# A fused Mamba and mixture-of-experts kernel: the order of the work between the last scan and the first expert tile

## The chip, the cores and the metric

The kernel runs on 1 core of one Trainium2 chip. The metric is the device time of one execution in microseconds (us). The five engines are TensorE (PE), VectorE (DVE), ScalarE (ACT), GpSimd (POOL) and SyncE (SP), which issues most of the DMAs. Each works through its own queue of instructions in program order, and they are tied together by semaphores.

## The reference

The input x is 2 x 2048 x 128 in fp32. Cut to what matters:

```python
# layer 1: Mamba block, with residual, then LayerNorm
h  = layernorm(x) * gamma + beta
u, z = split(h @ in_proj.T)                       # 256 channels each
uc = silu(causal_conv4(u) + conv_b)
dt, Bm, Cm = split(uc @ x_proj.T)
delta = softplus(dt @ dt_proj.T + dt_proj_b)
state = exp(delta * A) * state + delta * Bm * uc   # scan over 2048 steps, 256 x 16 states
y  = (state * Cm).sum(-1) + uc * D
x1 = layernorm(x + (y * silu(z)) @ out_proj.T + x)
# layer 2: mixture of experts, top 2 of 8, with residual, then LayerNorm
p  = softmax(x1 @ Wg + bg);  p_k, idx_k = top_k(p, 2)
eo = gelu(x1 @ W1[e] + b1[e]) @ W2[e] + b2[e]
out = layernorm(x1 + sum_k p_k * eo[idx_k])
```

## The kernel before, in words

The 4096 tokens are cut into 8 units of 512 (4 groups of 128 rows). The Mamba part runs as 8 "hosts", one for each unit: function `host(j)` exists once for each engine, and each engine's copy is its own instruction order written out by hand. In host j the scan of unit j is the backbone, 32 steps of 128 x 512, four to a quad; hung between its steps are the projections of later units and the back part of earlier ones.

**The scan's own loop.** SP spreads `du` into `flow` (L371); PE spreads delta into four banks (L805); ACT turns them into decays (L1136); DVE multiplies the inflow (L1378) and scans (L1395, 128 x 512 a step); POOL multiplies two finished steps with C in one instruction, `times_c` (L554, `hc`), so that a host has 16 such "slots" on POOL; PE adds the states up (`add_states`, L814). The last state of a unit feeds `post` on DVE (L1403), `out_proj` on PE (L828), `residual` and `back_stats` on DVE (L1409, L1304, L1308), `back_rstd` on POOL (L518 to L523), `xns` on ACT (L1146), `xn_T` on PE (L837), `xnT_evac` on ACT (L1152) and `logits` on PE (L844).

**Routing.** `best_two` (L1421 to L1431) and `one_hots` (L1437, L1443) on DVE find the two experts of each row; `shift_ex` (L571, POOL) and `gate_exp` (L1156, ACT) prepare the gate's softmax; `ranks` on PE (L858, L860) and on DVE (L1450, L1453) counts the rows ahead of each one; `mask_ranks` (L577, POOL), `place` (L1457 to L1463, DVE) and `places` (L582, POOL) make each row's place in an expert's list. `tag_rows` (L584 to L594, POOL) writes four numbers behind each row: its index (L589), its first expert (L590), its first probability (L591) and the difference of the two (L592, L594). Of these only the last three instructions need the exponentials' sum, `erec`. `list_rows` (L596 to L603, POOL) then scatters 128 rows into the lists `xs` in DRAM with one indirect DMA (L601); a unit needs eight. The one before it, `carrier` (L600), is there for its waits.

In host j the lists of unit j-2 are written after slots 11, 12, 13 and 14, two at each, and `back_rstd(j-1)` stands behind slot 8. After the last host come, on POOL, the routing and lists of unit 6 (with `back_rstd(7)` between the fourth and the fifth list), then those of unit 7. On DVE the order after the last scan is `ranks(6)`, `place(6)`, `post(7, 1)`, `residual(7)`, and so on to `place(7)`, and behind it 14 small `plan` instructions (L1526 to L1541) that turn the counts into a table of 71 tiles. On PE it is `add_states`, `ranks(6)`, `out_proj(7)`, `xn_T(7)`, `logits(7)`, `ranks(7)`.

**Experts.** 71 tiles of 128 rows follow. SP loads the weights W1 of three tiles ahead (L460), then waits for all lists to be in DRAM and loads the rows (L466): six tiles of rows are issued before the W1 of the fourth. For each tile PE transposes it (L988), multiplies by W1 (`hidden`, L995), ACT takes Gelu (L1279), PE multiplies by W2 (`output`, L1003), DVE scales, POOL scatters the result (L680). PE runs `x_T(n)`, `hidden(n-1)`, `output(n-2)` in turn. The first Gelu carries an ACT_TABLE_LOAD, since exponentials used another table before. A final part of 8 units adds the two halves and normalizes.

**Filling matmuls.** `idle` (L698) and `keep_busy` (L850) are matmuls on constants (128 x 512 bf16) whose result nobody reads; there are 36 and 130 of them, all before the last host.

Of the kernel before, what the change touches and what calls it, by code (L numbers as in the profile page):

```python
# [6 lines left out]
ACT = mybir.ActivationFunctionType  # L7
# [65 lines left out]
def mamba_moe(nc, consts, bcsel, du_d, xs, results, x, ln_gamma, ln_beta, in_proj_w, conv_w, conv_b, x_proj_w,  # L73
              dt_proj_w, dt_proj_b, A_log, Dskip, out_proj_w, Wg, bg, W1, b1, W2, b2, out):
    with ExitStack() as ctx:
# [34 lines left out]
        ones = sb("ones", [P, P], BF16)  # L110
# [19 lines left out]
        scrap = sb("scrap", [P, TT])  # L130
# [373 lines left out]
        def _(pool):  # L504
# [64 lines left out]
            def shift_ex(u):  # L569
                pool.wait_ge(s_top, u + 1)  # L570
                nc.gpsimd.tensor_tensor(ex[:], top[:], top[:, :, 0:1].broadcast_to([P, TT, E]), ALU.subtract)\  # L571
                    .then_inc(s_exs, 1)

            def mask_ranks(u):
                pool.wait_ge(s_rk, u + 1)
                for k in range(2):
                    ins = nc.gpsimd.tensor_tensor(masked[:, k], oh[:, k], rank[:], ALU.mult)  # L577
                ins.then_inc(s_ma, 1)
# [2 lines left out]
                pool.wait_ge(s_pf, u + 1)  # L581
                nc.gpsimd.tensor_copy(pos[u % 2][:], posf[:]).then_inc(s_po, 1)  # L582

            def tag_rows(u):  # L584
                pool.wait_ge(s_xn, u + 1)
                pool.wait_ge(s_er, u + 1)
                pool.wait_ge(s_ti, u + 1)
                row = xn[u % 2]
                nc.gpsimd.tensor_scalar(row[:, :, D], idc, float(T * u), None, ALU.add).then_inc(s_row, 1)  # L589
                nc.gpsimd.tensor_copy(row[:, :, D + 1], topi[:, :, 0]).then_inc(s_row, 1)  # L590
                nc.gpsimd.tensor_tensor(row[:, :, D + 2], ex[:, :, 0], erec[:], ALU.mult).then_inc(s_row, 1)  # L591
                nc.gpsimd.tensor_tensor(second[:], ex[:, :, 1], erec[:], ALU.mult).then_inc(s_row, 1)  # L592
                pool.wait_ge(s_row, 5 * u + 4)
                nc.gpsimd.tensor_tensor(row[:, :, D + 3], second[:], row[:, :, D + 2], ALU.subtract).then_inc(s_row, 1)  # L594
# [10 lines left out]
            def host(j):  # L605
                late = j + 1 < UNITS
                for slot in range(2 * QUADS):
                    times_c(QUADS * j + slot // 2, slot % 2)
                    if slot == 12 and j + 3 < UNITS:
                        front_rstd(j + 3)  # L610
                    if j == 0 and slot == 1:
                        front_rstd(2)
                    if slot == 7 and late and j >= 1:
                        add_log(j + 1)
                    if slot == 9 and late:
                        less_negative(j + 1)
                    if slot == 10 and late:
                        delta_u(j + 1)
                    if slot == (5 if j else 7) and late:
                        relu_plus_exp(j + 1)  # L620
                    if j >= 2:
                        if slot == 1:
                            shift_ex(j - 2)
                        if slot == 3:
                            mask_ranks(j - 2)
                        if slot == 6:
                            places(j - 2)
                            tag_rows(j - 2)
                        if slot in (11, 12, 13, 14):
                            first_row = 2 * (11, 12, 13, 14).index(slot)  # L630
                            list_rows(j - 2, first_row)
                            list_rows(j - 2, first_row + 1)
                    if slot == 8 and j >= 1:
                        back_rstd(j - 1)
# [23 lines left out]
                host(j)  # L658
            last = UNITS - 1
            shift_ex(last - 1)  # L660
            mask_ranks(last - 1)
            places(last - 1)
            tag_rows(last - 1)
            for n in range(TT):
                list_rows(last - 1, n)
            back_rstd(last)
            for n in range(TT, 2 * TT):
                list_rows(last - 1, n)
            shift_ex(last)
            mask_ranks(last)  # L670
            places(last)
            tag_rows(last)
            for n in range(2 * TT):
                list_rows(last, n)

# [19 lines left out]
        def _(pe):  # L695
# [125 lines left out]
            def out_proj(u, ts):  # L821
                mbank = fbank[fill_of(u, "out") % 2]
                if 0 in ts:
                    front_bank(u, "out")
                    pe.wait_ge(s_yd, 2 * u + 2)
                for t in ts:
                    for h in range(HALVES):
                        ins = nc.tensor.matmul(mbank[:, P * t:P * t + P], yg[:, h, P * t:P * t + P], woutT[:, h, :],  # L828
                                               start=(h == 0), stop=(h == 1))
                if TT - 1 in ts:  # L830
                    ins.then_inc(s_ff, 1)
# [20 lines left out]
            def ranks(u):  # L852
                o = front_bank(u, "ranks")
                pe.wait_ge(s_tk, u + 1)
                for t in range(TT + 1):
                    oo = o[:, E * t:E * t + E]
                    for s in range(t):
                        ins = nc.tensor.matmul(oo, ones[:], taken[:, s, :], start=(s == 0), stop=(t == TT and s == TT - 1))  # L858
                    if t < TT:
                        nc.tensor.matmul(oo, below[:], taken[:, t, :], start=(t == 0), stop=True)  # L860
                ins.then_inc(s_ff, 1)

            def host(j):
                late, early = j + 1 < UNITS, j + 2 < UNITS
                for g in range(STEPS):
                    if g % 2 == 0:
                        spread_pair((STEPS * j + g) // 2)
                    if g >= 11 and g % 4 == 3:
                        add_states(QUADS * j + (g - 11) // 4)
                    if g in (3, 7) and j >= 1:  # L870
                        add_states(QUADS * j + (g - 11) // 4)
                    if g == 28:
                        add_skip(j, 1)
                    if j == 0:
                        first_host(g)
                        if g == 31:
                            spread_b(1)
                        continue
                    if late:
                        if g == 1:  # L880
                            proj_dt(j + 1, 0)
                        if g == 2:
                            proj_dt(j + 1, 1)
                        if g == 4:
                            spread_c(j + 1)
                    if g == 5 and j >= 2:
                        ranks(j - 2)
                    if early:
                        if g == 6:
                            xhat_T(j + 2)  # L890
                        if g in (8, 9, 10, 12):
                            conv_u(j + 2, 0, ((8, 9, 10, 12).index(g),))
                    if g == 13:
                        add_skip(j, 0)
                    if g == 14:
                        out_proj(j - 1, (0, 1))
                    if g == 16:
                        out_proj(j - 1, (2, 3))
                    if early:
                        if g in (17, 18, 20, 21):  # L900
                            conv_u(j + 2, 1, ((17, 18, 20, 21).index(g),))
                        if g == 22:
                            proj_z(j + 2, 0)
                        if g == 24:
                            proj_z(j + 2, 1)
                    if g == 25:
                        xn_T(j - 1)
                    if g == 28:
                        logits(j - 1)
                    if early:  # L910
                        if g == 29:
                            proj_x(j + 2, (0,))
                        if g == 30:
                            proj_x(j + 2, (1,))
                    if late and g == 31:
                        spread_b(j + 1)
                    if early and g in KEPT_BUSY:
                        times, what, ahead = KEPT_BUSY[g]
                        keep_busy(fill_of(j + ahead, what), times)
# [57 lines left out]
            add_states(QUADS * UNITS - 2)  # L977
            add_states(QUADS * UNITS - 1)
            ranks(last - 1)
            out_proj(last, (0, 1, 2, 3))  # L980
            xn_T(last)
            logits(last)
            ranks(last)

            def x_T(n):
                pe.wait_ge(e_g[n % 8], 16 * (n // 8 + 1))
# [34 lines left out]
        def _(act):  # L1021
# [249 lines left out]
            xns(last)  # L1271
            xnT_evac(last)
            gate_exp(last)

            def gelu(n, e):
                act.wait_ge(e_h, n + 1)
# [18 lines left out]
        def _(dve):  # L1295
# [209 lines left out]
            for j in range(UNITS):  # L1505
                host(j)
            last = UNITS - 1
            ranks(last - 1)
            place(last - 1)
            post(last, 1)  # L1510
            residual(last)
            back_stats(last)
            best_two(last)
# [137 lines left out]
```

## Time and profile before

| | us |
|---|---|
| three executions | 778.39, 779.25, 782.07; median 779.25 |
| the profiled execution | 782.08, its span 780.3 |
| DVE, PE, POOL busy | 662.5, 602.2, 577.6 |
| last scan ends | 559.88 |
| first transpose of an expert tile | 601.66 |
| first result tile added at the end (L1590) | 754.38 |

The profiled execution is 1.8 us longer than its span, which is what lies outside the first and the last instruction. Times of the trace count from the span's start. In the timeline, a line stands for instructions of one kind that follow each other: start, duration of the whole group, engine, source line, operation, output and inputs with their sizes, how many, and in brackets how long the engine was idle before it and what ended that.
### The profile page before, as it was taken

What the parts mean: (1) busy time and instruction counts of PE and PEld (TensorE: products, weight loads), DVE (VectorE), ACT (ScalarE), POOL (GpSimd) and SP (SyncE); (2) the same over time, 40 slices, a digit from 0 to 9 for tenths busy, and PEclk for the clock granted to TensorE, in tenths of its full rate; (3) what the DMA queues carried; (4) which work ended last, traced back from release to release, by engine and by line L of the source; (5) the groups of instructions that cost most, each with busy time, mean ns of one, the idle gap of its engine ahead of it and who ended that gap; (6) DMA issues with size and microseconds to landing.
All of it is one profiled execution on the core that took longest, in us unless ns stands there. A gap on an engine that the chain in (4) does not pass through costs nothing. (4 is left out here: it accounts for less than half of the span.)

```text
span 780.3 us, 11886 instructions
## 1 busy us (share of the span) xinstructions
PE 602.2 (77%) x3071; PEld 293.7 (38%) x3071; DVE 662.5 (85%) x1343; ACT 434.3 (56%) x892; POOL 577.6 (74%) x544
## 2 busy tenths in 40 slices
PE   9768888987987888898798676685431999999920
PEld 4322222322322322232232122121131999998920
DVE  4288999999999999999998999999633788886855
ACT  3758587578467576657746644334110656554625
POOL 4345787976999899899899989968765456664644
PEclk9889999999999999999999987767755999999975
DMA  3095386577669668657656764954003677776754
GB/s 94 17 226 136 81 188 162 122 164 160 142 158 256 138 150 202 144 122 180 145 135 140 164 155 103 209 127 104 25 29 114 183 204 203 216 209 171 197 166 175
DMA packets 51169, 117.34 MB, mean 150 GB/s; under 512 B 8816, under 2 KB 25008, under 8 KB 43040
## 3 DMA queue, kind: packets, MB, share of 16 engines
q1 hardware_dynamic: 45344, 107.20, 56.4%
q0 software_dynamic: 4320, 8.99, 3.6%
q8 instruction: 26, 0.43, 0.3%
q10 hardware_dynamic: 1440, 0.40, 0.2%
q14 instruction: 39, 0.32, 0.2%
HBM read 100.21 MB, written 16.35 MB: 149 GB/s over the span
## 5 line engine op out<-in xcount | busy, mean ns | idle before, releaser
L554 POOL TENSOR_TENSOR hc<-hs,Crep 128x1024 f32<-128x1024 f32 x128 | 301.1, 2359 | 72.3 <-DVE hs L1395 51.3
L1395 DVE TENSOR_TENSOR_SCAN hs<-bank,state,flow 128x512 f32<-128x512 f32 x256 | 312.8, 1267 | 15.7 <-ACT bank L1136 7.5
L1136 ACT ACTIVATE bank<-bank,negA 128x512 f32<-128x512 f32 x256 | 164.6, 660 | 168.2 <-PE bank L805 158.8
L805 PE MATMUL bank<-delta,sel 64*128 64x512 f32 x512 | 157.5, 694 | 85.5 <-DVE hs L1395 83.6
L1378 DVE TENSOR_TENSOR flow<-flow,bank 128x2048 f32<-128x2048 f32 x63 | 142.8, 2266 | 0.0
L1279 ACT ACTIVATE flow<-bank,b1T 128x128 f32<-128x128 f32 x284 | 81.2, 369 | 58.0 <-issue 31.1
L805 PEld LDWEIGHTS bank<-delta,sel 64*128 64x128 f32 x512 | 42.3, 201 | 179.0 <-DVE hs L1395 149.3
L680 POOL DMA_INDIRECT results<-flow,idn x71 | 70.0, 985 | 33.1 <-issue 31.3
L814 PE MATMUL bank<-hc,kc 128*32 128x512 f32 x512 | 73.2, 646 | 10.8 <-POOL hc L554 10.8
L995 PE MATMUL bank<-flow 128*128 128x128 f32 x568 | 78.6, 283 | 1.9 <-DVE flow L1546 1.6
L1003 PE MATMUL bank<-w_sb,flow 128*128 x568 | 76.0, 277 | 1.6 <-ACT flow L1279 1.3
L601 POOL DMA_INDIRECT xs<-xn,pos x64 | 64.0, 1001 | 16.0 <-issue 15.9
L995 PEld LDWEIGHTS bank<-flow 128*128 128x128 f32 x568 | 71.4, 197 | 3.4 <-DVE flow L1546 2.0
L742 PE MATMUL bank<-hT,wtapT 128*128 128x512 f32 x128 | 69.1, 657 | 2.8 <-ACT hT L1040 1.5
L1003 PEld LDWEIGHTS bank<-w_sb,flow 128*128 128x128 f32 x568 | 69.9, 194 | 2.2 <-issue 2.2
L679 POOL TENSOR_TENSOR carrier<-kc 128x1 f32<-128x1 f32 x71 | 13.2, 186 | 35.3 <-DVE flow L1573 22.5
L742 PEld LDWEIGHTS bank<-hT,wtapT 128*128 128x128 f32 x128 | 22.2, 197 | 41.5 <-issue 33.9
L1546 DVE COPY flow<-bank 128x128 f32<-128x128 f32 x71 | 20.7, 292 | 19.0 <-PE bank L988 13.0
L850 PE MATMUL bank<-idle_rhs,ones 128*128 128x512 bf16 x130 | 33.3, 382 | 2.8 <-ACT pre L1050 1.2
L988 PE MATMUL bank<-ident,xg 128*128 128x128 f32 x71 | 19.9, 280 | 18.1 <-DMA xg<-xs 18.1
L1566 DVE TENSOR_TENSOR flow<-bank,b_rep 128x128 f32<-128x128 f32 x71 | 20.6, 291 | 13.8 <-PE bank L1003 9.1
L814 PEld LDWEIGHTS bank<-hc,kc 128*32 128x32 f32 x512 | 10.4, 111 | 56.8 <-issue 38.9
(198 smaller groups left out, 806.3 us busy)
## 6 DMA issues: line engine op xcount, KB each, us to landing
flow<-du_d SPq DMA_DIRECT2D x63, 1024.0 KB
flow<-L_ffn_W SPq DMA_DIRECT2D x71, 256.0 KB
xg<-xs SPq DMA_DIRECT2D x71, 66.0 KB
du_d<-du SPq DMA_DIRECT2D x28, 128.0 KB
xin<-L_attn_x SPq DMA_DIRECT2D x8, 256.0 KB, 3.3
hs<-results SPq DMA_DIRECT2D x8, 256.0 KB, 4.4
out<-hc SPq DMA_DIRECT2D x8, 256.0 KB, 2.0
results<-flow,idn POOLq DMA_INDIRECT x71
```

What stands on the lines that cost most here:

```text
L554: nc.gpsimd.tensor_tensor(hc[:, Q % 2, two, :], hs[:, Q % 2, two, :], Crep[u % 3][:].unsqueeze(1).broadcast_to([P, 2, T]), ALU.mult).then_ ...
L601: nc.gpsimd.indirect_dma_start(out=xs, out_offset=bass.IndirectOffsetOnAxis(ap=pos[u % 2][:, n:n + 1], axis=0), in_=xn[u % 2][:, n % TT, : ...
L680: nc.gpsimd.indirect_dma_start(out=results, out_offset=bass.IndirectOffsetOnAxis(ap=idn[:, n % 8:n % 8 + 1], axis=0), in_=ybuf[:, n % 8, : ...
L742: ins = nc.tensor.matmul(o[:], wtapT[:, h, k, :], hT[u % 2][:, k:k + T], start=(k == 0), stop=(k == TAPS - 1))
L805: ins = nc.tensor.matmul(dbank[2 * odd + i][:], sel[rows, odd, q % 4, :], delta[u % 2][rows, q // 4, :])
L814: ins = nc.tensor.matmul(ybank[32 * j:32 * j + 32, :], fold[:, q % 4, :], hc[:, Q % 2, j, :], start=(q % 4 == 0), stop=(q % 4 == 3))
L995: ins = nc.tensor.matmul(h_bank[n % 2][:, P * k:P * k + P], w1r[n % 4][:, P * k:P * k + P], xTs[:, n % 2, :])
L1003: ins = nc.tensor.matmul(o_bank[n % 2][:, 0:D], hTs[:, n % 2, k, :], w2_sb[:].rearrange("p e k d -> p (e k d)")[:, bass.ds(e * (HK * D) + ...
L1136: nc.scalar.activation(dbank[G % 4][:], dbank[G % 4][:], ACT.Exp, scale=negA[:, ch:ch + 1]).then_inc(s_ex, 1)
L1279: ins = nc.scalar.activation(hTs[:, n % 2, k, :], h_bank[n % 2][:, P * k:P * k + P], ACT.Gelu, bias=b1T[:, bass.ds(e * HK + k, 1)])
L1378: nc.vector.tensor_tensor(flow[Q % 3][:], flow[Q % 3][:], Brep[:].unsqueeze(1).broadcast_to([P, 4, T]), ALU.mult).then_inc(s_bu, 1)
L1395: nc.vector.tensor_tensor_scan(hs[:, Q % 2, j, :], dbank[G % 4][:], flow[Q % 3][:, j, :], state[:, Q // QUADS % 2, Q % QUADS, j:j + 1], AL ...
```

## The change

Six edits, each in the hand-written order of one engine:

- POOL: `tag_rows` is cut in two. `name_rows` (index and first expert) waits for `s_xn` and `s_ti`; `weigh_rows` (probabilities) waits for `s_er`. In the hosts they stand one behind the other as before; after the last host `name_rows` moves ahead of `mask_ranks`.
- POOL: in the last host alone (`late` is false) the lists stand behind slots 8 to 11, not 11 to 14. The two lists of slot 8 come ahead of `back_rstd`.
- DVE: after the last scan `post(last, 1)` stands ahead of `ranks(last - 1)` and `place(last - 1)`.
- PE: `idle_tail` issues 5 filling matmuls ahead of the last `out_proj`, 30 ahead of `xn_T(last)`, and 64 behind `ranks(last)`, ahead of the first tile. They wait for nothing and write a bank that nobody reads then.
- ACT: behind the last `gate_exp` a Gelu of four numbers a partition, which nobody reads.

```diff
-            def tag_rows(u):
+            def name_rows(u):
                 pool.wait_ge(s_xn, u + 1)
-                pool.wait_ge(s_er, u + 1)
                 pool.wait_ge(s_ti, u + 1)
                 row = xn[u % 2]
                 nc.gpsimd.tensor_scalar(row[:, :, D], idc, float(T * u), None, ALU.add).then_inc(s_row, 1)
                 nc.gpsimd.tensor_copy(row[:, :, D + 1], topi[:, :, 0]).then_inc(s_row, 1)
+
+            def weigh_rows(u):
+                pool.wait_ge(s_er, u + 1)
+                row = xn[u % 2]
                 nc.gpsimd.tensor_tensor(row[:, :, D + 2], ex[:, :, 0], erec[:], ALU.mult).then_inc(s_row, 1)
...
-                            tag_rows(j - 2)
-                        if slot in (11, 12, 13, 14):
-                            first_row = 2 * (11, 12, 13, 14).index(slot)
+                            name_rows(j - 2)
+                            weigh_rows(j - 2)
+                        listing = (11, 12, 13, 14) if late else (8, 9, 10, 11)
+                        if slot in listing:
+                            first_row = 2 * listing.index(slot)
...
             shift_ex(last - 1)
+            name_rows(last - 1)
             mask_ranks(last - 1)
             places(last - 1)
-            tag_rows(last - 1)
+            weigh_rows(last - 1)
...
             shift_ex(last)
+            name_rows(last)
             mask_ranks(last)
             places(last)
-            tag_rows(last)
+            weigh_rows(last)
...
+            def idle_tail(times):
+                for _ in range(times):
+                    nc.tensor.matmul(dbank[3][:], ones[:], idle_rhs[:])
...
             ranks(last - 1)
+            idle_tail(5)
             out_proj(last, (0, 1, 2, 3))
+            idle_tail(30)
             xn_T(last)
             logits(last)
             ranks(last)
+            idle_tail(64)
...
             gate_exp(last)
+            act.wait_ge(s_scrap, 2)
+            nc.scalar.activation(scrap[:], minus_half[:], ACT.Gelu).then_inc(s_scrap, 1)
...
             last = UNITS - 1
+            post(last, 1)
             ranks(last - 1)
             place(last - 1)
-            post(last, 1)
```

## Rows read from the trace of the kernel before

**Rows 1.** The page, the span in 40 slices of 19.5 us: the granted clock.

```profile
PEclk9889999999999999999999987767755999999975
```

**Rows 2.** Timeline of the last host, 530 to 563 us: POOL, and DVE's one-hots and last scan.

```profile
530.40 2.34 POOL L554 TENSOR_TENSOR hc<-hs,Crep 128x1024 f32<-128x1024 f32 x1 [0.67 <-DVE hs L1395]
...
534.71 2.36 POOL L554 TENSOR_TENSOR hc<-hs,Crep 128x1024 f32<-128x1024 f32 x1
...
546.33 2.34 POOL L554 TENSOR_TENSOR hc<-hs,Crep 128x1024 f32<-128x1024 f32 x1 [0.27 <-DVE hs L1395]
...
551.12 2.36 POOL L554 TENSOR_TENSOR hc<-hs,Crep 128x1024 f32<-128x1024 f32 x1
...
555.62 2.77 DVE L1437 TENSOR_TENSOR oh<-kc,topi 128x64 f32<-128x64 f32 x1
555.94 2.36 POOL L554 TENSOR_TENSOR hc<-hs,Crep 128x1024 f32<-128x1024 f32 x1
...
558.61 1.27 DVE L1395 TENSOR_TENSOR_SCAN hs<-bank,state,flow 128x512 f32<-128x512 f32 x1
```

**Rows 3.** Timeline, the one-hots of an earlier host, beside no multiplication on POOL.

```profile
435.37 0.20 DVE L1437 TENSOR_TENSOR oh<-kc,topi 128x64 f32<-128x64 f32 x1
```

**Rows 4.** Timeline behind the last scan, 563 to 570 us.

```profile
563.17 1.94 PE L814 MATMUL bank<-hc,kc 128*32 128x512 f32 x8 [8.56 <-POOL hc L554]
...
565.88 0.46 POOL L577 TENSOR_TENSOR masked<-oh,rank 128x32 f32<-128x32 f32 x2 [2.57 <-DVE rank L1450]
...
566.51 0.68 DVE L1403 TENSOR_TENSOR yg<-bank,gated 128x512 f32<-128x512 f32 x1
566.66 0.19 POOL L582 CAST pos<-posf 128x8 uint32<-128x8 f32 x1 [0.32 <-DVE posf L1463]
...
567.34 3.75 PE L828 MATMUL bank<-woutT,yg 128*128 128x128 f32 x16 [1.77 <-DVE yg L1403]
567.40 0.20 POOL L591 TENSOR_TENSOR xn<-ex,erec 128x4 f32<-128x4 f32 x1
...
568.86 1.08 POOL L601 DMA_INDIRECT xs<-xn,pos  x1 [0.48 <-issue]
```

**Rows 5.** The chain that ended last, 577 to 603 us: start, duration, what.

```profile
577.57 1.10 PE bank L837 x4
...
581.31 0.20 DVE lg L1421
...
583.77 0.20 DVE rank L1450
...
584.85 0.17 POOL pos L582
...
587.96 1.08 POOL xs L601
...
600.56 1.69 DMA xg<-xs
```

**Rows 6.** Timeline of the last unit's logits and of the first expert tiles.

```profile
579.42 1.85 PE L844 MATMUL bank<-wg_sb,xnT 128*128 128x8 f32 x8 [0.77 <-ACT xnT L1152]
...
602.57 2.03 PE L995 MATMUL bank<-flow 128*128 128x128 f32 x8
...
604.64 0.33 SPq L460 DMA_DIRECT2D flow<-L_ffn_W  x1
604.71 1.28 ACT L1279 ACT_TABLE_LOAD   x1 [22.22 <-PE bank L995]
...
607.29 1.15 PE L1003 MATMUL bank<-w_sb,flow 128*128 x8 [0.78 <-ACT flow L1279]
```

**Rows 7.** Timeline, four transposes, six filling matmuls and eight logits elsewhere, at clock 1.00.

```profile
9.85 0.66 PE L717 MATMUL bank<-ident,xhat 128*128 128x128 f32 x4
10.35 1.46 PE L698 MATMUL bank<-idle_rhs,ones 128*128 128x512 bf16 x6
...
548.31 0.95 PE L844 MATMUL bank<-wg_sb,xnT 128*128 128x8 f32 x8
```

## The prediction

> **What bounds the kernel now.** I read the slices first: the granted clock is high through most of the program, sags from 0.8 to 0.5 towards the end of the Mamba part, and is back at 0.9 for the experts [rows 1]. Then the chain that ended last: between the last scan and the first expert tile it is one thread through PE, DVE, POOL and ACT, then eight lists on POOL, the landing and the first row load [rows 5]. Nothing overlaps there that matters, so what leaves this thread leaves the time. Then the timeline, in three parts: the last host, where POOL's multiplications stand in line with its lists [rows 2]; the stretch from the last added states to the lists of unit 6, where POOL and PE run side by side [rows 4]; and the first tiles, where PE works at 1.2 GHz and waits for a table load [rows 6]. Behind them PE paces 71 tiles and none of the edits touches it. So only the stretch 530 to 608 us is costed.
>
> **1. Lists three slots sooner.** Prices: a multiplication 2.36; two lists 551.12 - (546.33 + 2.34) = 2.45 [rows 2]; the first pair with its carrier I take as 0.3 more; `back_rstd` 534.71 - 532.74 = 1.97 [rows 2]. From slot 8 at 530.40 I add: slot 8 to 532.8, its lists to 535.5, `back_rstd` to 537.4, slot 9 to 539.8, lists to 542.2, slot 10 to 544.6, lists to 547.0, slot 11 to 549.4, lists to 551.9, then slots 12, 13, 14 back to back to 554.2, 556.6 and 558.9. If nothing else held slot 15 it would end at 561.3 where it now ends at 563.1, when PE can add the last states [rows 4], a gain of 1.8. But slot 15 needs the last scan, and before the last scan DVE has the one-hots. They cost 0.20 on their own [rows 3], and 2.77 here: recorded from 555.62, they end at 558.39, just behind the multiplication that POOL began at 555.94, 0.3 us after them [rows 2]. POOL kept a DVE instruction with two SBUF inputs out although DVE was first on record. In the new order slots 13 and 14 run back to back over exactly this moment. If POOL keeps DVE out until it has to stop, the one-hots end at 559.1, the one-hots' sum takes 0.2, the last scan (1.27 [rows 2]) ends at 560.6, and slot 15 at 563.0: gain 0.1. Bounds: 0 and 1.8. I take 0.1, because the row shows POOL winning against an earlier DVE instruction, and put 1.8 with the rivals.
>
> The Trainium skill (SBUF — State Buffer, section "SBUF: two separate sides") states that the shared port pair is an exclusive lock and that whichever of the two starts first gets it for its whole instruction. The blocking agrees with the trace (2.77 against 0.20); "first" does not by the recorded starts. By the page the waiting one-hots would go in when slot 13 ends, and the sum would be 1.7 better; that is the first rival.
>
> The two lists and their DMAs also pass `back_rstd(6)`: it ends at 537.4, 2.7 later than 534.7, and ACT's `xns(6)` (at 536.69 before) follows 0.7 later, with one decay behind it. The scan that needs this decay started 0.8 after it; I cost this at 0, and at 0.7 if that cover is gone.
>
> **2. `post` first, `name_rows` first (unit 6).** POOL sits idle for 2.57 before the masks [rows 4], so the two `name_rows` instructions cost nothing there. From `pos` to the third tag instruction it is 567.40 - 566.66 = 0.74 now, and 0.28 without the two: 0.46 off. `post` (0.68) goes ahead of the ranks on DVE; it can start when the states are added at 563.17 + 1.94 = 565.1, while the masks were released by a rank that ended 565.8, so the rank is now written at 566.1 and POOL's path starts 0.3 later. Net for the lists of unit 6: -0.15. On the other side `yg` is ready at 565.9, but PE now has 5 fillers first, 2.1 us at 1.2 GHz (0.43 each, twice the 0.216 of 2.4 GHz: six take 1.46 [rows 7], one alone 0.38, so five steps 1.08). `out_proj` starts at 567.7, 0.35 late; if the clock rises half way through it ends near 570.4, 0.7 early; without a rise 0.35 late. That hardly matters: `back_rstd` stands behind four lists on POOL, whose end moves only by 0.15, and moves with it. Term: -0.15, bounds 0 and -0.3.
>
> **3. Fillers before `xn_T`.** It starts at 577.57 [rows 5]. 30 x 0.216 = 6.5 from 570.4 ends at 576.9, before 577.4 when the rows are there; if the clock rises only at 572 they end at 578.2. Cost 0, bound +0.8. What they give: four transposes 0.66 instead of 1.10, -0.43; eight logits 0.95 instead of 1.85, -0.90 [rows 5, 6, 7]. Ranks perhaps 0.1. Term: -1.4, bounds +0.8 and -1.5.
>
> **4. `name_rows` ahead for unit 7.** From `pos` (584.85) to the first list (587.96) it is 3.1 [rows 5]. Unhindered, without the two, it would be 0.28 + (568.86 - 567.40) = 1.74 [rows 4]. DVE's plan instructions run beside it from here on, and one with two SBUF inputs can hold POOL as POOL held the one-hots: I take 2.1. Term -1.0, bounds -0.8 and -1.4. The first two tags now sit beside the ranks, where POOL waits.
>
> To the first tile: 0.1 + 0.15 + 1.4 + 1.0 = 2.6 sooner. The lists themselves (1.27 apart, eight) and the DMAs stay. SP's own work, the eight tails and W1, moves with the plan, 2 us sooner too, and is off the thread.
>
> **5. The table and the clock at the first tile.** The table load of 1.28 [rows 6] moves into ACT's idle 22.22. At 1.2 GHz PE is busy with `hidden(1)` until 606.5 and idle only 0.78 before `output(0)` [rows 6], so the table alone gives 0.8. With the clock high as well: eight products take 0.9 (1.15 recorded at the high clock, with its fixed part, against 2.03 for `hidden(0)` [rows 6]), so `hidden(0)` ends at 603.4, Gelu (1.3, from the table load's end at 605.99 to 607.29) at 604.7, `hidden(1)` at 604.4, and `output(0)` runs 604.7 to 605.6. Now it runs 607.29 to 608.2 [rows 6]. Term -2.55. It needs the clock high at the tile. The 64 fillers are 13.8 us at 2.4 GHz; the ranks end 583.7 [rows 5] - 1.5 = 582.2, so they end at 596.0, and the tile comes at 599.1: 3 us of idle PE, less if part of them ran at 1.2 GHz. I take the full term, bound -0.8. Next in line is SP: the W1 of tile 3 is issued behind six row loads, at 604.64 [rows 6], and is needed now at about 607.6 (two tiles of 1.9 behind 605.6, less the first product) and not 610.2; enough for one transfer that took 1.69 for a quarter of the bytes [rows 5], with little to spare.
>
> **Sum.** -2.6 - 2.5 = -5.1. Against the profiled execution's own 782.08 that is 777.0. That run lies 2.8 above the median of 779.25, and nothing in this stretch explains it, so I take the sum off the median: 774.1.
>
> **The rivals.**
> - **The one-hots slip in between slots 13 and 14.** For it: two engines ask for a port and one has waited a microsecond. Against: [rows 2]. A further -1.7: 772.4. Chance 0.27.
> - **The clock falls again before the first tile.** For it: in the profile before it fell while PE waited for POOL at the end of the last host, 8.56 idle [rows 4], and it stays at 0.5 in the slices of the lists [rows 1]; 3 us of idle stand between the fillers and the tile. Only the table's 0.8 is left of 2.55: 775.9. Chance 0.25.
> - **Slower: the fillers run at 1.2 GHz throughout.** Then 30 take 12.9 from 571.5 and hold `xn_T` to 584.3, 6.8 late; the 64 take 27.4 and end near 618, 16 after the first tile could start: 779.25 + 16 - 0.8 = 794.5. It turns to a loss from the point where the 64 last longer than the roughly 17 us between ranks and tile. Against: the same matmuls ran at 0.216 at the start. A milder form, one late rise at each place, costs about 2 and lands at 776.5. Chances 0.04 and 0.09.
>
> The Trainium skill (TensorE: Matmul & The Clock Gate, "Wait — 56ns, not 53.3ns?") gives 426.7 ns cold and 215.7 ns warm between such matmuls; the second agrees with the 0.216 of [rows 7].
>
> **How the numbers follow.** The forecast itself has 0.35. A measurement of this kernel can tell about 0.5%, 3.9 us, so faster means under 775.4. Of the forecast 0.85 is under it, of the first rival nearly all, of the second two fifths, of the mild late rise a quarter: 0.30 + 0.26 + 0.10 + 0.02 = 0.68. Slower than 783.1 is the full filler case and a little: 0.05. The rest, 0.27, is the same. The range goes from the first rival with the tags at their best, 770.9, to the second with `xn_T` held up and no rise in the logits, 777.5.
>
> **What would show it.** Right: the last `hc` ends within 0.2 of 563.1 and the one-hots last over 3 us; `xn_T` starts near 577.4 with logits at 0.95; from `pos` to the first list 2.1; the first tile near 599; its `hidden` at clock 1.00 and no table load behind it. Wrong: fillers that end after the rows are there, at either place; an idle PE behind the third tile waiting for W1; slots 12 to 15 that end at 561.3; a `hidden` of 2 us again.

## The result, and the profile after

The changed kernel takes 775.96 us (median of 13 runs, 774.21 to 779.22); the kernel before takes 782.07 (median of all its 13 runs). The two medians lie 6.1 us apart. One of the executions of the kernel before, at 803.29, was a slow one; the ratio, 0.9932 with a 95% interval of 0.9916 to 0.9949, leaves it out, and that is 5.3 us less. A second series of the same kernel gave 0.9942 (0.9925 to 0.9959), 4.5 us less. The forecast was 5.1 us less, and 774.1 with a range of 770.9 to 777.5.

The page of the changed kernel, the slices that answer to [rows 1]:

```profile
PEclk9889999999999999999999986857878999999975
```

The two slices of 0.5 that covered the way to the first expert tile are gone; what remains low lies inside the last hosts and in one stretch between the fillers.

The timeline of its last host, which answers to [rows 2]:

```profile
529.73 2.34 POOL L554 TENSOR_TENSOR hc<-hs,Crep 128x1024 f32<-128x1024 f32 x1 [0.76 <-DVE hs L1411]
...
551.24 6.94 POOL L554 TENSOR_TENSOR hc<-hs,Crep 128x1024 f32<-128x1024 f32 x3
...
554.97 3.31 DVE L1453 TENSOR_TENSOR oh<-kc,topi 128x64 f32<-128x64 f32 x1
...
558.41 1.28 DVE L1411 TENSOR_TENSOR_SCAN hs<-bank,state,flow 128x512 f32<-128x512 f32 x1
...
559.77 2.34 POOL L554 TENSOR_TENSOR hc<-hs,Crep 128x1024 f32<-128x1024 f32 x1 [1.59 <-DVE hs L1411]
```

Slots 12, 13 and 14 run without a gap, 6.94 for three. The one-hots of DVE, issued at 554.97, end at 558.28, which is 0.1 behind the end of the third of them. The end of slot 13, at 555.8, fell into their wait and did not let them in. Then comes the last scan, and POOL waits 1.59 for it.

The timeline behind the last scan, which answers to [rows 4]:

```profile
562.39 0.24 POOL L588 TENSOR_SCALAR xn<-kc 128x4 f32<-128x4 f32 x1
...
564.17 0.69 DVE L1419 TENSOR_TENSOR yg<-bank,gated 128x512 f32<-128x512 f32 x1 [4.48 <-PE bank L821]
...
565.83 0.19 POOL L582 CAST pos<-posf 128x8 uint32<-128x8 f32 x1 [0.32 <-DVE posf L1479]
...
566.51 2.94 PE L835 MATMUL bank<-woutT,yg 128*128 128x128 f32 x16
...
567.43 1.08 POOL L604 DMA_INDIRECT xs<-xn,pos  x1 [0.48 <-issue]
...
569.29 6.42 PE L872 MATMUL bank<-idle_rhs,ones 128*128 128x512 bf16 x29
...
572.38 0.23 POOL L518 TENSOR_SCALAR cveps<-cmv 128x4 f32<-128x4 f32 x1
...
576.15 0.63 PE L844 MATMUL bank<-ident,xn 128*128 128x128 f32 x4 [0.43 <-ACT xn L1160]
```

The first `name_rows` instruction sits in POOL's idle time at 562.39. From `pos` to the first list it is 1.60 (2.20 before [rows 4]). `out_proj` takes 2.94 for 3.75, since the clock rises inside it. The 30 fillers (one is missing from this trace, as from the 64 below) end at 575.7, 0.43 ahead of the transposes, so they hold nothing up, and the four transposes take 0.63 at the high clock.

The chain that ended last, which answers to [rows 5]:

```profile
578.61 0.20 DVE lg L1437
...
581.07 0.20 DVE rank L1466
...
582.13 0.19 POOL pos L582
...
582.48 0.39 POOL second L595
...
583.98 1.23 POOL xs L604
...
593.10 2.93 DMA xs<-xn,pos
...
597.38 1.84 DMA xg<-xs
```

From `pos` to the first list it is 1.85 for 3.1, and POOL was held up once on the way (`second` 0.39). The last scatter's landing takes 2.93, which nobody had forecast; in the chain of the kernel before the same piece took 2.28.

The timeline of the fillers and the first tiles, which answers to [rows 6]:

```profile
579.93 1.28 ACT L1289 ACT_TABLE_LOAD   x1
...
580.89 16.31 PE L872 MATMUL bank<-idle_rhs,ones 128*128 128x512 bf16 x63
...
598.32 0.33 PE L1002 MATMUL bank<-ident,xg 128*128 128x128 f32 x1 [1.12 <-DMA xg<-xs]
...
599.44 1.06 PE L1009 MATMUL bank<-flow 128*128 128x128 f32 x8
...
600.65 2.18 ACT L1295 ACTIVATE flow<-bank,b1T 128x128 f32<-128x128 f32 x8 [19.22 <-PE bank L1009]
...
601.93 1.15 PE L1017 MATMUL bank<-w_sb,flow 128*128 x8 [0.43 <-ACT flow L1295]
```

The table load stands at 579.93 under idle time. The fillers take 16.31 and not the 13.8 of the high clock. The stretches of the changed kernel show why (the clock is the third number from the right):

```profile
572.00:578.00 6.00, 4.80 (x27) 2.47 (x25) 0.00 (x0) 2.23 (x5) 4.92 (x8) 1.00 0.10 34
...
580.00:585.00 5.00, 4.48 (x24) 1.87 (x25) 3.92 (x14) 1.42 (x2) 3.09 (x10) 0.50 0.08 23
...
587.00:598.00 11.00, 10.15 (x47) 4.41 (x45) 0.86 (x4) 0.00 (x0) 5.54 (x6) 1.00 0.50 147
```

The clock fell behind the logits, during TensorE's wait for the routing (the last product ends at 578.57, and the granted clock is 0.50 from 579.0), and rose again under the fillers (1.00 from 585.75). They ended about 1.1 ahead of the first transpose, and `hidden(0)` ran at 1.06.

**One ruler for all kernels.** What lies behind the first output product differs between executions of one and the same kernel: 173.0 and 170.1 us in two profiles of the kernel before, 173.3 and 168.4 in two of the changed one. So the edits are read from the stretch between the start of slot 8 in the last host and the first output product, which repeats within 0.1. Its parts, from the starts in the timelines: A slot 8 to the end of slot 15; B from there to `xn_T(7)`; C to `lg`; D to the first list of unit 7; E first to last list; F to the first tile's transpose; G to the first output product.

| kernel | A | B | C | D | E | F | G | sum |
|---|---|---|---|---|---|---|---|---|
| before | 32.72 | 14.45 | 3.74 | 6.65 | 8.98 | 4.72 | 5.63 | 76.89 |
| before, again | 32.74 | 14.46 | 3.74 | 6.65 | 8.98 | 4.71 | 5.68 | 76.96 |
| changed | 32.38 | 14.04 | 2.46 | 5.37 | 9.12 | 5.22 | 3.61 | 72.20 |
| changed, again | 32.34 | 14.01 | 2.46 | 5.37 | 9.12 | 5.26 | 3.58 | 72.14 |

The change gives 4.7 us here: 0.34 in A, 0.41 in B, 1.28 in C, 1.28 in D and 2.02 in G, less 0.14 in E and 0.50 in F.

### The profile page after: what moved, and what is told of

Same layout as the page of the kernel before. It is cut to its first block and busy times, and to the rows that moved or that the text cites. A ratio compares the mean times of both kernels' runs of the same rounds, so it can differ in the third digit from the quotient of the medians.

```text
span 775.2 us, 12066 instructions
## 1 busy us (share of the span) xinstructions
PE 620.2 (80%) x3151; PEld 298.5 (39%) x3170; DVE 662.5 (85%) x1343; ACT 434.5 (56%) x893; POOL 576.5 (74%) x544
## 5 line engine op out<-in xcount | busy, mean ns | idle before, releaser
L821 PE MATMUL bank<-hc,kc 128*32 128x512 f32 x512 | 74.8, 659 | 9.6 <-POOL hc L554 9.6
L1009 PE MATMUL bank<-flow 128*128 128x128 f32 x568 | 75.6, 276 | 2.3 <-issue 2.1
L1009 PEld LDWEIGHTS bank<-flow 128*128 128x128 f32 x568 | 69.0, 192 | 3.4 <-issue 2.8
L857 PE MATMUL bank<-idle_rhs,ones 128*128 128x512 bf16 x115 | 29.9, 380 | 5.5 <-ACT relu L1102 1.7
L1589 DVE SCALAR_TENSOR_TENSOR flow<-xg,is_first,flow 128x128 f32<-128x128 f32 x71 | 24.9, 351 | 2.7 <-DVE flow L1586 0.2
```

Of the source, the lines that this page charges most:

```text
L821: ins = nc.tensor.matmul(ybank[32 * j:32 * j + 32, :], fold[:, q % 4, :], hc[:, Q % 2, j, :], start=(q % 4 == 0), stop=(q % 4 == 3))
L1009: ins = nc.tensor.matmul(h_bank[n % 2][:, P * k:P * k + P], w1r[n % 4][:, P * k:P * k + P], xTs[:, n % 2, :])
```

## The experiments

Ratios are to the kernel before, in interleaved runs, each series on one chip. Sums and parts are those of the ruler; the changed kernel has 72.20 and 72.14.

**The kernel before, once more** (no edit).

> The kernel before, once more, as a profile taken beside the next three. Both theories: from the end of slot 15 to the first output product 44.2 us, as in the first profile of it (607.29 - 563.12), the clock at 0.50 there; only the part behind the first tiles may differ, if that is what makes the totals of the two chips differ by 5 us.

Measured: 44.22 from slot 15 to the first output product (607.84 - 563.62), and all seven parts within 0.05. Behind it, 170.1 for 173.0. The ruler holds for the stretch that the edits touch; the totals differ elsewhere.

**The changed kernel, once more** (no edit).

> The changed kernel once more, beside the next three. Both theories: ratio to the kernel before 0.993, slot 8 to slot 15's end 32.4 us, from there to the first output product 39.8.

Measured: ratio 0.9942 (0.9925 to 0.9959), parts within 0.04 of the first profile.

### Who holds the last scan

**The one-hots behind the last scan.**

```diff
-                    if g == 30 and j == UNITS - 1:
+                    if g == 31 and j == UNITS - 1:
                         one_hots(j - 1)
```

> The changed kernel with the one-hots of unit 6 behind the last scan on DVE, not ahead of it. Theory (POOL's back-to-back multiplications keep DVE's one-hots out, and so hold the last scan and slot 15): the last scan ends some 3 us sooner, slot 15 follows slot 14 without a gap, so the 1.59 us in which POOL waited go: 1.6 us faster than the changed kernel, ratio to the kernel before 0.991. The one-hots are then held until slot 15 ends, 2 to 5 us long, and cost nothing, because TensorE needs them only behind the last added states. Rival (the last scan is late for another reason, the decay or a buffer): slot 15 ends where it did, 12.4 us behind the start of slot 12's neighbour as in the changed kernel, gain under 0.3 us.

Measured: ratio 0.9916 (0.9896 to 0.9936); A 30.71 for 32.34 to 32.38; sum 70.48. Its timeline:

```profile
552.44 9.23 POOL L554 TENSOR_TENSOR hc<-hs,Crep 128x1024 f32<-128x1024 f32 x4
...
557.36 4.40 DVE L1453 TENSOR_TENSOR oh<-kc,topi 128x64 f32<-128x64 f32 x1
...
561.73 1.94 PE L821 MATMUL bank<-hc,kc 128*32 128x512 f32 x8 [2.66 <-POOL hc L554]
```

Four slots now follow each other in 9.23, and the one-hots are held for 4.40, over the end of slot 14 (559.4) and until slot 15 ends (561.68). This hurts nobody. The theory's 1.6 is there (1.65), the rival is out.

**POOL waits for the one-hots.**

```diff
+                    if slot == 14 and not late:
+                        pool.wait_ge(s_oh, UNITS - 1)
                     times_c(QUADS * j + slot // 2, slot % 2)
```

> The changed kernel, but POOL waits for the one-hots ahead of slot 14 of the last host. If a waiting GpSimd lets the port go, the one-hots enter as slot 13 ends and take about 0.2 us beyond it; the last scan then ends 2 us sooner and slot 15 starts directly behind slot 14: POOL loses 0.3 us at the wait and wins 1.6, so 1.3 us faster than the changed kernel. Rival (the one-hots are slow by themselves in this place, not held by POOL's stream): they still last 3 us or more, slot 14 starts 1.6 us late, and slot 15 ends no sooner, or 1 us later.

Measured: ratio 0.9915 (0.9896 to 0.9933); A 30.94, 1.42 less than the changed kernel. Its timeline:

```profile
550.98 4.64 POOL L554 TENSOR_TENSOR hc<-hs,Crep 128x1024 f32<-128x1024 f32 x2
...
554.73 0.98 DVE L1455 TENSOR_TENSOR oh<-kc,topi 128x64 f32<-128x64 f32 x1
...
555.79 4.66 POOL L554 TENSOR_TENSOR hc<-hs,Crep 128x1024 f32<-128x1024 f32 x2 [0.17 <-DVE oh L1455]
```

The same one-hots in the same place, issued at the same point of POOL's stream, last 0.98 and end 0.1 behind slot 13, because POOL stops there. So an added wait takes 1.4 us out of A. It was POOL's unbroken stream that kept the port, and not the one-hots' own length. The sum is 71.36, only 0.8 under the changed kernel, since F is 5.70 and G 3.77. In G something of the prediction's second rival shows: the fillers ended 2.52 ahead of the tile, the granted clock was 1.00 until 599, 0.57 from 599 to 600 and 0.50 behind it, and the first output product took 1.86 for 1.15.

**The lists behind slots 11 to 14 again.**

```diff
-                        listing = (11, 12, 13, 14) if late else (8, 9, 10, 11)
+                        listing = (11, 12, 13, 14)
```

> The changed kernel with the last host's lists behind slots 11 to 14 again. Theory (the one-hots' wait for the port swallows what the earlier lists gain): slot 15 ends no more than 0.4 us later than in the changed kernel, measured from the start of slot 8, and the total is 0 to 0.4 us longer. Rival (the earlier lists work as meant): 1.6 us or more longer.

Measured: ratio 0.9947 (0.9930 to 0.9963); A 32.73, 0.37 longer than the changed kernel. The theory's bound of 0.4 holds. The sum is 72.73; beside A, F is 0.3 longer (5.57, see below) and G 0.1 shorter.

**Lists late and one-hots behind.** Both edits above.

> The last host's lists behind slots 11 to 14 and the one-hots behind the last scan. Theory (two limits, each hiding the other: with late lists slot 15 waits for POOL's lists, with early lists for the last scan): the last scan ends 2.8 us sooner but slot 15 still stands behind two lists, so it ends where it did in the kernel with late lists, within 0.3 us, and the 1.3 to 1.6 us that the same move gave with early lists are absent. Rival (moving the one-hots is worth something by itself): 1 us or more faster than with late lists alone.

Measured: ratio 0.9924 (0.9907 to 0.9942); A 32.70, as with late lists alone. Its timeline:

```profile
557.33 2.44 DVE L1411 TENSOR_TENSOR_SCAN hs<-bank,state,flow 128x512 f32<-128x512 f32 x2
...
562.65 0.96 POOL L604 DMA_INDIRECT xs<-xn,pos  x1 [0.31 <-issue]
563.64 2.35 POOL L554 TENSOR_TENSOR hc<-hs,Crep 128x1024 f32<-128x1024 f32 x1
```

The last scan is done at 559.77 and slot 15 begins at 563.64, directly behind a list. The move that gives 1.65 with early lists gives 0.03 with late ones; early lists give 0.37 with the one-hots in the old place and 1.99 (32.70 - 30.71) with them behind. The sum, 71.84, is 0.9 under that of late lists, all of it in F (4.74 for 5.57), which is not what was moved.

### What the fillers and the table are worth

**No fillers.** The three `idle_tail` calls are left out.

> The changed kernel without its 5, 30 and 64 filling matmuls; all else stays. Theory (the fillers raise the clock, and that is worth something at the last unit's transposes and logits and at the first tiles): the granted clock is 0.50 from the last host until after the first tile; the four transposes take 1.1 and the eight logits 1.85 as before, so logits come 1.3 us later behind the xn rows; hidden(0) takes 2.0, and from the first tile's transpose to the first output product it takes some 1.2 us longer than the 3.6 of the changed kernel. Total +2.5 us against the changed kernel, so about 3 us faster than the kernel before (ratio 0.996). Rival (the clock rises by itself or the fillers delay as much as they give): within 1 us of the changed kernel, ratio 0.993.

Measured: ratio 0.9951 (0.9932 to 0.9970). C 3.74 as before, G 4.44, sum 73.84, 1.64 to 1.70 more than the changed kernel. Its timeline:

```profile
579.38 1.85 PE L851 MATMUL bank<-wg_sb,xnT 128*128 128x8 f32 x8 [0.77 <-ACT xnT L1163]
...
601.52 1.99 PE L1006 MATMUL bank<-flow 128*128 128x128 f32 x8
```

The fillers give 1.28 at the logits and 0.85 at the tiles. The expected 2.5 were too many: F is 4.84 here and not 5.2, and G loses 0.85 and not 1.2. B is 14.00 as with fillers, so the quicker `out_proj` gave nothing by itself. Nor was the clock at 0.50 throughout, as expected: it was at 1.00 from 572 to 574, behind `out_proj`, and back at 0.52 from 574 to 576, ahead of the transposes.

**No early table load.** The Gelu of four numbers is left out.

> The changed kernel without the Gelu of four numbers that loads the table early. Theory: the table load of 1.28 comes back behind the first hidden product, at a place where TensorE already waits for the first Gelu (0.43 us), so the first output product starts 1.28 us later and the time is 1.3 us longer than the changed kernel's. Rival (as with the low clock of the kernel before, where only 0.8 was exposed): +0.4 to +0.8 us.

Measured: ratio 0.9948 (0.9930 to 0.9966); G 4.66. Its timeline:

```profile
600.16 1.07 PE L1009 MATMUL bank<-flow 128*128 128x128 f32 x8
...
601.34 1.28 ACT L1292 ACT_TABLE_LOAD   x1 [20.22 <-PE bank L1009]
...
603.92 1.15 PE L1017 MATMUL bank<-w_sb,flow 128*128 x8 [1.70 <-ACT flow L1292]
```

From `hidden(0)` to the first output product it is 3.76, in the changed kernel 2.49 (601.93 - 599.44): 1.27 more, and PE's idle time goes from 0.43 to 1.70. (All of G is only 1.05 to 1.08 longer, since `hidden(0)` started 0.90 and not 1.1 behind the first transpose here.) The table alone, at the low clock, is the row of the kernel without fillers: G 4.44 against 5.63, 1.19; 0.26 of it are not the table's, because the clock rose within `hidden(1)` there, which took 1.66 for 1.92. The two together give 2.02 to 2.10, less than 1.19 and the 1.0 of the clock alone (4.66 against 5.63 to 5.68) would add up to, but only by 0.1 to 0.2.

**40 fillers for 64 ahead of the first tile.**

> 40 fillers ahead of the first tile for 64. Theory (the clock falls again in a long gap): the fillers end near 592, 6 us ahead of the first transpose; the granted clock falls to 0.50 in the gap, hidden(0) takes 2.0 for 1.06 and the first output product comes 0.8 to 1.0 us later than in the changed kernel. Rival (once raised, the clock lasts until the tile): hidden(0) 1.06, no difference.

Measured: ratio 0.9947 (0.9927 to 0.9968); G 4.75. Its stretches and its timeline:

```profile
592.00:596.00 4.00, 1.00 (x5) 0.27 (x3) 0.00 (x0) 0.00 (x0) 2.44 (x3) 1.00 0.78 248
596.00:598.00 2.00, 0.00 (x0) 0.00 (x0) 0.00 (x0) 0.00 (x0) 0.00 (x0) 0.71 0.00 1
598.00:603.00 5.00, 3.73 (x17) 3.44 (x17) 1.77 (x11) 0.93 (x4) 0.00 (x0) 0.50 0.38 84
```

```profile
598.88 0.48 PE L1002 MATMUL bank<-ident,xg 128*128 128x128 f32 x1 [5.88 <-DMA xg<-xs]
...
600.01 1.91 PE L1009 MATMUL bank<-flow 128*128 128x128 f32 x8
```

With PE idle for 5.88 the clock fell ahead of the tile, and G is 1.15 longer than in the changed kernel. It fell at 596.8, 3.8 behind the last filler. This is the mechanism of the prediction's second rival. In the changed kernel the gap was 1.1; at the high clock throughout, the 64 would have left one of 3.6 (598.32 - 580.89 - 13.8). Whether the clock had fallen in that one no run shows: it held through gaps of 1.92 and 2.13 (the kernel with the one-hots behind, and that with late lists) and fell within the first tiles behind one of 2.52 (where POOL waits).

**90 fillers for 64.**

> 90 fillers ahead of the first tile for 64. Theory (fillers are in TensorE's order and nothing may pass them): 26 more at 0.216 are 5.6 us, of which the gap of 1.1 before the first transpose takes some; the first output product comes 4.0 to 4.6 us later, at a high clock, and the total is 4 us longer, ratio 0.998. Rival (the tiles are paced by the row loads or by SP behind the first, and catch up): the delay at the first transpose is 4.5 but shrinks to under 2 us by the end.

Measured: ratio 0.9972 (0.9954 to 0.9991); F 8.84, G 3.24, sum 75.35, 3.2 more than the changed kernel; the median of 776.55 is 3.7 above the 772.88 of the changed kernel in the same series. The tile's transpose starts directly behind the last filler, at 603.00. The delay stays in the total, so the tiles don't catch up; its size is 1 us under the 4.0 to 4.6 expected: 26 fillers are 5.6, of which 1.1 went into the gap; the first fillers spent less time at the low clock in this profile than in that of the changed kernel; and 0.35 came back in G, since the row loads had all landed.

### Where part F comes from

The kernel with 90 fillers apart, F is 4.7 to 5.0 in seven profiles and 5.2 to 5.7 in six. SP's W1 loads lie nearer to the last scatter than before: they start 4.3 ahead of its issue before (592.65 and 596.94) and 3.1 ahead in the changed kernel (590.00 and 593.10), since the lists came forward by more than SP, which works through its eight tail writes first.

**Two W1 loads ahead of the lists' end.**

```diff
-            for n in range(3):
+            for n in range(2):
                 load_w1(n)
...
             for n in range(3):
                 load_tile(n)
+            load_w1(2)
```

> The changed kernel with two W1 loads ahead of the lists' end instead of three; the third is issued behind the first three row loads. Theory (the W1 loads now lie over the last scatter and lengthen its landing, 2.3 to 2.9 us): the last scatter lands within 2.5 us and the first transpose comes 0.4 us sooner after it; the total gains 0.2 to 0.4 us, too little for the total to show. Rival (the landing varies by itself): 2.9 as in the changed kernel. Either way a W1 of tile 3 issued 0.8 us later could leave TensorE waiting at the fourth tile; then up to 0.5 us is lost there.

Measured: ratio 0.9936 (0.9916 to 0.9957); the last scatter's landing in the chain:

```profile
593.69 2.34 DMA xs<-xn,pos
```

F is 4.85, G 3.34, sum 71.50, 0.64 to 0.70 less than the changed kernel; the total can't show so little. But it is not a clean proof: the kernel without fillers, the one with 40 and the one with late lists and the one-hots behind have three W1 loads at the same distance of 3.1 and landings of 2.40, 2.41 and 2.39. What they share is that SP's issues of W1 took 2.0 to 2.1, while they took 2.8 to 3.0 in the kernels with landings of 2.6 to 3.15. The kernel in which POOL waits has 2.0 and 3.41, at a distance of 1.85. So neither the number of loads nor the distance alone orders these landings, and the cause of the longer F stays open.

### A version that is faster than both

**One-hots behind, `back_rstd` one list sooner, 26 fillers for 30.**

```diff
-            for n in range(TT):
+            for n in range(TT - 1):
                 list_rows(last - 1, n)
             back_rstd(last)
-            for n in range(TT, 2 * TT):
+            for n in range(TT - 1, 2 * TT):
                 list_rows(last - 1, n)
```

> The changed kernel with the one-hots behind the last scan, back_rstd of the last unit ahead of the fourth list of unit 6 instead of behind it, and 26 fillers ahead of xn_T for 30. Theory: with the one-hots 1.5 us; back_rstd waited 0.9 us for the fourth list after its moments were ready, which go, so xn_T starts 0.8 us sooner; together 2.3 us faster than the changed kernel, ratio to the kernel before 0.990 or a little under. Rival (the fourth list, now behind back_rstd, pushes the lists of unit 6 into the path of unit 7, or the fillers end late): no faster than with the one-hots alone.

Measured: 769.77 us, ratio 0.9888 (0.9872 to 0.9904); A 30.71, B 12.76 (14.04 in the changed kernel), sum 69.20. Its timeline:

```profile
569.59 0.96 POOL L604 DMA_INDIRECT xs<-xn,pos  x1 [0.30 <-issue]
570.02 0.38 DVE L1324 BATCH_NORM_AGGREGATE cmv<-cst 128x2 f32<-128x6 f32 x4
570.62 0.22 POOL L518 TENSOR_SCALAR cveps<-cmv 128x4 f32<-128x4 f32 x1
```

The third list ends at 570.55, the moments at 570.40, and `back_rstd` starts right behind the list. It gains 1.27, one list, where 0.8 were expected: the moments were ready sooner than I had counted, because `out_proj` took 2.33 here and 2.94 in the profile that I had counted from (granted clock 0.83 for 0.63 over it). The lists of unit 6 still end long before those of unit 7.

## Why the prediction was right, point by point

**The sum was right** (5.1; the ruler shows 4.7, the two series 5.3 and 4.5), and every step took effect in the forecast direction. That the sizes agree so closely is in part luck: steps 1, 2 and 4 gave 0.8 more than forecast, steps 3 and 5 with E and F gave 1.3 less.

**The level was less sure than the difference.** 774.1 was taken off the median of three executions, 779.25; the median of 13 is 782.07, off which the same sum gives 777.0. The measured 775.96 lies between. The 0.68 for "faster" was set at 775.4, from the same three executions: the median misses that line, while the ratio, with an upper bound of 0.9949, passes the 0.5% that the line stood for. The low end of the range, 770.9, does not come out of its terms, which add up to about 771.8 (774.1 less 1.7, 0.4 and 0.15).

- **Step 1, the lists sooner: 0.1 forecast, 0.34 to 0.40 measured, of 1.8 that the sum of POOL's work allowed.** The step's reading was right: the one-hots were kept out until POOL had to stop. It put slot 15's end at 563.0, 32.6 behind slot 8; it came at 32.4, because the one-hots end 0.1 behind slot 14 and not 0.2, and the sum of the one-hots is done 0.1 sooner. `xns(6)`, at 536.76 against a shifted 536.02, was 0.7 late as forecast and cost nothing.
- **The first rival fell** with the same rows. By the prediction's reading of the page's rule (the Trainium skill, SBUF — State Buffer, "SBUF: two separate sides": whoever starts first has the pair for the whole instruction) it should have come true. The trace agrees that a GpSimd instruction keeps VectorE out; what the next owner is when a GpSimd instruction ends and the next one is ready, the section does not say, and the prediction took it to be DVE. 0.98 with a stop behind slot 13, 3.31 and 4.40 without one: here POOL kept it over one of its own ends, with DVE waiting. The prediction's other argument, that DVE was first on record by 0.3 in the kernel before, is weak: the record of the one-hots begins at 555.62, before the scan ahead of them ends (554.44 + 1.26 = 555.70), so their recorded start does not tell when they asked for the port.
- **Step 2: 0.15 forecast, 0.41 measured.** The forecast let `post` push the ranks by 0.3; from slot 15's end to `pos` it is 3.72 for 3.54, so 0.18. The two tags moved away gave 0.60 and not 0.46: from `pos` to the first tag that is left it is 0.15, not 0.28. That POOL's four lists, not `out_proj`, decide when `back_rstd` starts was right: 4.95 from the first list to `cveps` in both kernels, and B is the same without fillers.
- **Step 3: 1.4 forecast, 1.28 measured**, and the 30 fillers ended 0.43 before they would have cost something.
- **Step 4: 1.0 forecast, 1.28 measured**; one instruction of POOL was caught instead of more.
- **Step 5: 2.55 forecast, 2.02 to 2.10 measured.** The term was oversized at two places of 0.3 each. The second row's transpose came 0.95 behind the first one's (0.64 before), and `x_T(1)` stands ahead of `hidden(0)` in PE's order, so `hidden(0)` started 1.1 behind the first transpose and not 0.8. And Gelu started 1.21 behind `hidden(0)` (600.65 - 599.44), where the forecast let it start after the 0.9 of eight products. The table alone was undersized, 0.93 for 0.8, if the clock's 0.26 are taken off its 1.19. The W1 of tile 3 was in time.
- **The second rival** was nearer than its place in the text. The step had the clock high from the start of the 64; it fell behind the logits and came back under them, which stretched them by 2.5 and left a gap of 1.1 instead of 3.6. So the full term came with the help of a fall that the step had not foreseen; whether it would have come without it is not shown. The kernel with 40 shows the rival's price, 1.15.
- **The slower rival**: fillers do delay once they last too long (with 90 of them the tile came 3.6 later), but they raised the clock each time.
- **Not in the sum:** part E, 0.14 longer (the first list took 1.23 for 1.08), and part F, 0.5 longer. I had moved SP's loads with the plan and looked only for whether they were late, not for what they run beside; that this is the cause of F is not shown.

## What to carry to other kernels

Give every sum of a queue's work the question who may be waiting for a resource that this queue holds: with the lists gone from between POOL's multiplications DVE could no longer get in, and a move on the other engine, or one added wait, was worth four times what moving the lists gave (1.65 and 1.42 against 0.37). Two limits that hide each other have to be moved together: each alone gave 0.4 or 0.0, both 2.0. Fillers for the clock are sized by two measured gaps: too few and the clock falls again ahead of the work, too many and they are the delay; and their own speed depends on the clock that they find.

## What was not expected of the hardware

- GpSimd kept a VectorE instruction with two SBUF inputs out beyond the end of its own instruction, as long as the next one was ready (4.40 us beside 9.23 of back-to-back work); the same instruction takes 0.20 alone.
- The landing of the last scatter of 66 KB took 2.28 and 2.29 us with the W1 loads issued 4.3 ahead of it, 2.34 to 3.15 at 3.1, and 3.41 at 1.85; what made it vary at the same distance is open.
- The same expert phase of 71 tiles and what follows it took 168.4 and 173.3 us in two profiles of one kernel. In the longer one PE waited at five places behind the first output product, 4.3 us in total; in the shorter one at one, for 0.5. Why was not tried.
